# Two mixtures of experts, dense or on sorted rows, in a two-layer recurrent fp32 kernel

## The reference

```python
xn = layernorm(x)                       # x: 16 x 512 x 128
s  = quaternion_stack(xn)               # 4 layers: qkv, Hamilton products, spectral filter, projection, MLP
g  = silu(moe0(xn))                     # 8 experts, hidden 256, each token uses its best 2
x  = x + s * g
xn = layernorm(x)
s  = windowed_attention(xn)             # 16 heads of 64, windows of 128, rotary embedding
g  = silu(moe1(xn))                     # 32 experts, hidden 64, best 4 within 2 of 4 groups, plus a shared expert
x  = x + s * g

# moe0: for every expert e: h = silu(xt @ w_gate[e]) * (xt @ w_up[e]); out += ge[:, None] * (h @ w_down[e])
# moe1: y_e = (silu(xt @ gate_w[e].T) * (xt @ up_w[e].T)) @ down_w[e].T; sum of topk_w * y_e over the chosen 4, + shared
```

## Time and profile before

| | us |
|---|---|
| median of 3 runs | 4817.23 |
| lowest, highest | 4806.15, 4819.19 |
| profiled execution, its own time | 4814.87 |
| its span | 4813.1 |
| PE busy | 4264.2 (89%) |
| DVE busy | 3833.5 (80%) |
| ACT busy | 3274.9 (68%) |
| POOL busy | 1996.1 (41%) |
| a middle round | 287.7 |
| start to the end of the first round | 298.3 |
| last round | 199.5 |

### The profile page before, as it was taken

How to read it: one execution, slowest core, us unless ns; L and a number is a source line. 1 busy time by engine, 2 the same in 40 slices (tenths; PEclk the granted TensorE clock), 3 DMA queues, 4 the chain that set the end, 5 groups by cost and what they waited for, 6 DMA issues and landing times. The chain is left out here.

```text
span 4813.1 us, 75678 instructions
## 1 busy us (share of the span) xinstructions
PE 4264.2 (89%) x20208; PEld 2603.9 (54%) x20208; DVE 3833.5 (80%) x8946; ACT 3274.9 (68%) x6140; POOL 1996.1 (41%) x2033
## 2 busy tenths in 40 slices
PE   5669899898998989899898998989889898998979
PEld 3435555565554555555564554555555564555555
DVE  4779798887978879798887978889798887979853
ACT  2447677676776767677676776767777676777745
POOL 1234344344444444444443434444344443434423
PEclk8779999999999999999999999999999999999989
DMA  4001111111101101111111101101111111111100
GB/s 126 16 25 30 27 30 33 26 32 27 30 25 31 39 21 31 28 29 31 29 31 31 28 23 33 36 21 31 30 28 31 30 31 31 27 27 32 34 20 21
DMA packets 144530, 149.37 MB, mean 31 GB/s; under 512 B 27748, under 2 KB 107932, under 8 KB 143960
## 3 DMA queue, kind: packets, MB, share of 16 engines
q1 hardware_dynamic: 144088, 144.19, 11.5%
HBM read 22.45 MB, written 4.19 MB: 6 GB/s over the span
## 5 line engine op out<-in xcount | busy, mean ns | idle before, releaser
L644 POOL TENSOR_TENSOR s_h<-s_h,ge 128x512 f32<-128x512 f32 x512 | 696.9, 1361 | 1319.2 <-ACT ge L654 1076.0
L952 DVE TENSOR_TENSOR acc<-acc,tmp 128x512 f32<-128x512 f32 x768 | 610.6, 800 | 10.1
L952 DVE TENSOR_TENSOR tmp<-comps 128x512 f32<-128x512 f32 x768 | 605.4, 790 | 8.4
L776 ACT ACTIVATE s_h<-bG 128x512 f32<-128x512 f32 x528 | 314.8, 596 | 434.9 <-DVE hu L1139 226.5
L1371 PE MATMUL bC<-hu,w_d 128*128 128x512 f32 x1056 | 565.3, 617 | 15.7 <-DVE hu L1139 15.7
L753 ACT ACTIVATE probs<-bT,nmax 128x256 f32<-128x256 f32 x1024 | 410.8, 476 | 201.7 <-DVE nmax L1100 199.8
L631 POOL TENSOR_TENSOR rot<-rot,sinT 128x512 f32<-128x512 f32 x256 | 338.1, 1321 | 427.6 <-DMA rot<-raw 426.2
L1100 DVE TENSOR_REDUCE nmax<-bT 128x2 f32<-128x512 f32 x512 | 335.5, 685 | 225.8 <-PE bT L1284 225.2
L1326 PEld LDWEIGHTS bT<-V,probsT 128*128 128x128 f32 x3584 | 430.6, 192 | 101.4 <-issue 56.6
L1139 DVE TENSOR_TENSOR hu<-bU,s_h 128x512 f32<-128x512 f32 x528 | 361.4, 684 | 153.8 <-PE bU L1364 79.5
L1326 PE MATMUL bT<-V,probsT 128*128 128x65 f32 x3584 | 438.7, 274 | 26.7 <-ACT probsT L654 25.6
(11 more groups left out here) (201 smaller groups left out, 9482.7 us busy)
## 6 DMA issues: line engine op xcount, KB each, us to landing
rot<-raw SPq DMA_DIRECT2D x1024, 64.0 KB, 2.0
comps<-comps SPq DMA_DIRECT2D x384, 120.0 KB
x_ld<-in_L_attn_x SPq DMA_DIRECT2D x66, 128.0 KB, 2.2
comps<-comps SPq DMA_DIRECT2D x384, 8.0 KB
out<-O SPq DMA_DIRECT2D x16, 256.0 KB, 2.7
w_a<-in_L_attn_W_qkv SPq DMA_DIRECT2D x1, 1536.0 KB, 14.6
w_fc<-in_L_attn_fc_w SPq DMA_DIRECT2D x1, 1024.0 KB, 9.9
w_g<-in_L_ffn_w_gate SPq DMA_DIRECT2D x1, 1024.0 KB, 5.7
```

The costliest lines, as they stand in the source:

```text
L644: nc.gpsimd.tensor_tensor(s_h[:, :], s_h[:, :], ge[:, :], ALU.mult).then_inc(weighed, 1)
L776: nc.scalar.activation(s_h[:, :], bG[:, :], ACT.Silu).then_inc(silu, 1)
L952: V_.tensor_tensor(dst, i0, i1, op).then_inc(ham[h], 1)
```

## The change

Each mixture now works on the rows that were routed to an expert, and on no others.

- **Sort.** From the hits of the routing, PE counts for each expert and each token how many came before (bf16 matmuls with triangles of ones, `rank` and `base`), and DVE makes of it the slot of every choice, with each expert's rows padded to whole tiles of 128 rows, and the expert's number for each tile (`ids`). There are 15 tiles for mixture 0 and 47 (run as 12 groups of 4) for mixture 1.
- **Scatter.** POOL writes the normalised rows to `xs_d` in DRAM with indirect transfers, one for 128 rows: 8 for mixture 0 and 16 for mixture 1 (L702). SP loads them back in 16 groups of 4 tiles (L632), PE turns them (`xT`), ACT copies them to `xs_f`.
- **Weights by tile.** For every tile SP reads the expert's number into a register and issues a load of that expert's weights: 15 of 393 KB (L650, L651) and 48 of 128 KB (L658, L659), each mixture with three buffers.
- **Units.** A tile of mixture 0 is 4 gate and up matmuls of 128 columns and 2 for down, a group of mixture 1 is 8 of 128 columns (64 x 128 out) and 2 of 256. `hu` has two buffers. The sums go out by `ev` (ACT to `ys`), SP stores them in `ys_d` (L639), POOL gathers the rows again (8 and 16 indirect transfers, L710), and DVE weighs and adds them (`mix`), then ACT takes `silu`.
- **Gone:** the selector matmuls, `ge` and its copies, `s_h * ge` on POOL, the split into three parts, the four kinds of turns named above. `out` gives rows by token (32 matmuls of 128 columns in place of 8 of 512).
- **Start.** Weights come laid out by the host, so PE's turns and the ACT copies at the start go. 4.1 MB of `xs_d` are filled with zeros. The loads of the experts' weights into SBUF go.
- All strings of `ORDER` are new.

The diff, cut to its core (POOL, SP, DVE, PE in this order):

```diff
+TILES0, TILES1 = (SLOTS0 - E0) // P + E0, (SLOTS1 - E1) // P + E1
+GT = 4
+WB0, WB1 = 3, 3
+XB, YB = 4, 2
...
+            def scatter(l, n):
+                pool.wait_ge(sort_step[l], n * SORT_STEPS + 8)
+                pool.sem_inc(pool_go, 1)
+                src = xn if l == 0 else x1n
+                for t in range(NT):
+                    for k in range(KS[l]):
+                        at = t * KS[l] + k
+                        nc.gpsimd.indirect_dma_start(xs_d[l], bass.IndirectOffsetOnAxis(slot[l][:, at:at + 1], 0),
+                                                     src[:, t, :], None).then_inc(scattered[l], 16)
+            def gather(l):
...
+                        nc.gpsimd.indirect_dma_start(yg[l][:, k, t, :], None, ys_d[l],
+                                                     bass.IndirectOffsetOnAxis(slot[l][:, at:at + 1], 0)
...
-                def u_part(name, u):
-                    pool.wait_ge(silu, r.unit + (u + 1))
-                    pool.wait_ge(ge_sb, r.gel + (unit_kind(u)[4] + 1))
-                    nc.gpsimd.tensor_tensor(s_h[:, :], s_h[:, :], ge[:, :], ALU.mult).then_inc(weighed, 1)
...
+                def w_part(name, u):
...
+                        e = sp.value_load(ids[0][0:1, u:u + 1], min_val=0, max_val=E0 - 1)
+                        sp.dma_start(w_e0[:, u % WB0, :], p_e0[e]).then_inc(w_in[0][u % WB0], 16)
+                        return
...
+                    for k in range(GT):
+                        tile = min(n * GT + k, TILES1 - 1)
+                        e = sp.value_load(ids[1][0:1, tile:tile + 1], min_val=0, max_val=E1 - 1)
+                        sp.dma_start(w_e1[:, n % WB1, k, :], p_e1[k % 2][e]).then_inc(w_in[1][n % WB1], 16)
...
+                        V_.tensor_tensor(hu[:, n % 2, :], bG[:, S // 2:], s_h[:, 0:S // 2], ALU.mult).then_inc(h_ready, 1)
...
+                    if name == "mix":
...
+                        dve.wait_ge(gathered[n], 16 * K * NT * (no + 1))
+                        w = weight[n][:, :, :].rearrange("p t k -> p k t").unsqueeze(3).to_broadcast([P, K, NT, D])
+                        g = yg[n][:, :, :, :]
+                        V_.tensor_tensor(g, g, w, ALU.mult).then_inc(mix_step[n], 1)
...
-                        mm(bG[:, :], g, src[:, :], start=True, stop=True).then_inc(g_full, 1)
...
+                            for j in range(2 * HALF0):
+                                ins = mm(bG[:, j * P:(j + 1) * P], w[:, j * P:(j + 1) * P], tok, start=True, stop=True)
...
+                            for j in range(2):
+                                for k in range(GT):
...
+                                    ins = mm(bG[on, at:at + P], w_e1[:, buf, k, j * I1:(j + 1) * I1],
+                                             xs_f[:, g % 2, k * P:(k + 1) * P], start=True, stop=True)
...
```

More of the change, by code:

```diff
@@ L113, in has_work @@
         return False
-    if step[0] == "weight":
-        u = step[1]
-        if engine == "pool":
-            return u < UNITS - 1
-        return u < UNITS - 1 and (u >= UNITS0 or u % HALF0 == 0)
+    if engine == "dve" and step == ("gu", SHARED):
+        return False
     if engine == "act":
-        return step not in [("down", u) for u in range(UNITS) if u not in (UNITS0 - 1, UNITS - 1)] and \
-            (step[0] != "r0" or step[1] == 1)
+        return step[0] != "r0" or step[1] == 1
     return True
@@ new lines, in program, with fill_at @@
+        FILLS = NG + 1
+        BANK = NG + 2
+        PER_B = NG // XB
+        first = Round(0, None, 0, 0, 1, 0)
+        last = Round(None, NB - 1, (NB - 1) * UNITS, (NB - 1) * FILLS, (NB - 1) * BANK + 2, (NB - 1) * PER_B)
+        def middle(i):
+            return Round(i, i - 1, i * UNITS - (UNITS - TILES0), i * FILLS - (FILLS - G0), i * BANK - (BANK - G0 - 2),
+                         i * PER_B - (PER_B - G0 // XB))
+        def fill_at(g):
+            return G0 if g == "shared" else g + (g >= G0)
@@ L453, in rounds, with streams, part_of, part @@
             one(last)
-        def streams(r, a, t, u=None, rt=None):
-            units = units_of(r)
-            def u_part(name, n):
-                if n in units:
-                    u(name, n)
+        def streams(r, a, t, m=None, rt=None, x=None, w=None):
+            def part_of(f):
+                def part(*step):
+                    if in_round(r, step):
+                        f(*step)
+                return part if f is not None else None
             def r_part(name, n):
@@ L534, in _ @@
-            load(w_a1[:, :], w_qkv, loaded["wqkv"])
+            load(w_att[:, :, :, :], attn_w.rearrange("l k t n -> k l t n"), loaded["attn"])
+            load(w_fc[:, :, :], fc_w.rearrange("l k n -> k l n"), loaded["attn"])
+            sp.wait_ge(blank, 1)
+            for l in range(2):
+                n = xs_d[l].shape[0] // P * D
+                width = TOPK1 * NT * D
+                flat = xs_d[l].rearrange("(p a) d -> p (a d)", p=P)
+                for at in range(0, n, width):
+                    end = min(at + width, n)
+                    load(flat[:, at:end], yg[1][:, :, :, :].rearrange("p k t d -> p (k t d)")[:, 0:end - at], zeroed)
@@ L537, in _ @@
             load(cmod[:, :], c_cmod, cs)
+            load(w_mp[:, :, :, :], mproj_w.rearrange("l (a p) n -> p l a n", p=P), cs)
+            load(w_a1[:, :], w_qkv, loaded["wqkv"])
             load(cosT[:, :], c_cos, cs)
@@ L682, in _ @@
             prep_sig(R0_TOP)
-            for h in range(2):
-                prep_gates(h, prep_ready)
             def one(r):
```

819 lines of the change are left out of this document (479 added, 340 removed).

## The result

The changed kernel takes 5234.11 us (median, 5227.76 to 5242.23) against 4815.24 for the kernel before: a ratio of 1.087 (95% interval 1.085 to 1.090). I had forecast 4604. The profiled execution has a span of 5235.3 us, 422 more than before.

What follows compares the result with a forecast made beforehand. The prediction took a chain between DVE and PE as the bound, DVE's 238 us not shrinking. Terms of -12.6 us a round gave 275.1; with start, first and last rounds -211 from 4814.9: 4604 us, range 4520 to 4740.

Steps and rivals of the forecast that it cites:

- PE's work: PE in a middle round: 96 us of matmuls removed, 66.3 added, net -30, to 233 us.
- the clock: PE's granted clock may fall to 0.92: 10 us more PE work a round, of which a third shows.
- Waits of DVE on PE: DVE's waits for PE in a round shrink as mixture matmuls get shorter: -10 us, between 0 and -34.
- The wait on POOL's weighing: DVE's wait for POOL's s_h before hu goes: -4.6 us a round, called certain.
- the port: Port shared by DVE and POOL: POOL's s_h operation leaves, -2 us a round (gain at most 5.0, loss at most 2.2).
- Indirect transfers: 48 a round on POOL at t = 1.3 us each; bursts make gather 1 late, +3 us a round.
- Rival 2: Bursts on POOL: at 2.25 us a transfer, gather 1 and scatter 0 add 22.6 us a round, 4943 us; chance 0.13.
- Register reads on SP: 63 a round ahead of weight loads: 1.0 us a read, 1.6 a tile; SP 5 us late in mixture 1.
- rival 1: SP is the new bound: at 1.5 us a read, 22 us more a round, 4956 us; chance 0.17.
- the 4 us a round at the round's end: End of the round: mix 1 and sort 0 on DVE fall into existing waits, hiding 4 us: -4.
- Rival 3: Small matmuls on PE cost 1.45 times in bulk: +22 us, a round about 285, 4754 us; chance 0.07.
- The port rule: Skill's rule for GpSimd-issued transfers while VectorE holds the shared port: about 0.62 us alone, 3.1 beside a VectorE copy.

Runs made afterwards that it cites:

- e5_both: The changed kernel with no weights fetched in the rounds and plain transfers in place of indirect ones: 4819 us, against 5234 for the changed kernel.
- e13_l0cols: e5_both with 48 in place of 128 columns in the gate and up matmuls of mixture 0 only: 4909 us against 4819.
- e11_warm: e5_both with 16 idle fp32 matmuls of 128 columns added on PE at the start of each round: 4754 us against 4819.
- b2_cols: The kernel before with 352 in place of 512 columns in each gate, up and down matmul of the mixtures: 4781 us against 4815.
- b1_noweigh: The kernel before without POOL's weighing of the units (s_h times ge): 4791 us against 4815.
- e4_plain: The changed kernel with 12 plain transfers a round in place of 48 indirect ones for scatter and gather: 5032 us against 5234.
- e14_nobufwait: The changed kernel with small weight fetches sent to spare DRAM, so SP waits for no free buffer: 5479 us, against 5197 with small fetches that wait.

## Why the prediction was wrong, point by point

Three steps failed, and a fourth in part. The waits of DVE that I let fall with PE's and POOL's work were to give 16.6 us a round, and gave 3.2 where each was tested alone. The fetches cost 15.7 us a round, not 5, and the bursts 11.8, not 3. And the clock fell below the end of my range.

- **PE's work:** 233 us forecast. Measured 252 at a clock of 0.88; at the 0.97 of before that would be 229 (252 x 0.88/0.97, an estimate). The amount was about right, in part by luck, as its terms were not: eight matmuls of 64 output rows take 1.09 us, not 8 x 0.22, four of mixture 0 take 1.16, not 4 x 0.22.
- **The clock:** the term that failed most quietly. I had 0.92 and "a third shows" as an end of my own range. It came to 0.88. In e5_both it moved the time both ways, by +90 us in e13_l0cols and -65 in e11_warm, so less PE work may cost time. What it cost in after itself no run parts from the rest.
- **Waits of DVE on PE, -10 a round:** wrong. Matmuls cut by 27 us in the kernel before give 2.0 (b2_cols). I had divided the waits by PE's load. An in-order engine that waits for others itself has to be followed to what it waits for.
- **The wait on POOL's weighing, -4.6 "with certainty", and the port, -2:** -1.2 together (b1_noweigh). The wait was taken up by the next ones. DVE's operations do get shorter, and by more than I said: those with the same tiles and form, in the same number, take 15.4 us a round less after than before, `acc<-acc,tmp` at 512 columns a mean of 718 ns, not 800. But without the weighing alone it is 4.1 (b1_noweigh). Where the rest comes from, with all strings of `ORDER` new, is not shown. It ends up as idle time.
- **Indirect transfers:** t = 1.3 came out (0.97 + 0.30), by luck, as I had only taken it from another kind of operation. Their place was wrong. I weighed gather 1 and scatter 0. The wait of 6.0 us is at scatter 1, 16 transfers in the middle of layer 0, which I had not put against the root behind it. They are a term mis-sized: I had 3 us a round for all of them; e4_plain gives 11.8, and 27 in the last round, for which I had nothing. Rival 2 named the mechanism, but with a price of 2.25 a transfer as its condition, which was not needed.
- **Register reads on SP:** 1.0 was too much (0.45). Yet rival 1's mechanism is the larger half: 253 us, 15.7 a round where I had 5. I asked whether SP can issue all it has in the stretch; it can. What counts is what stands behind each fetch in the order: four tiles are 3.7 to 4.1 us, and a wait for a free buffer on top, ahead of a roll that DVE needs next. I wrote that it decides from a read of 1.3 us on. That threshold came from throughput and was wrong: a read of 0.45 us was enough.
- **Sum:** without the 8 us a round that I had allowed for fetches and bursts, 120 in 15 rounds, my sum would say 4484. e5_both, which has neither, takes 4819. The 630 us from the forecast to 5234 are thus 335 of base gain that was not there and 415 for fetches and bursts (253 and 202, 40 of it in common), less the 120. If b1_noweigh and b2_cols hold for the new kernel too, the waits explain 13.4 us a round or 201 of the 335 (an estimate). The rest stays open: the 4 us a round at the round's end and the 12 of the last round (it took 202.1 us in e5_both, 199.5 before) were not tested alone, and the clock of e5_both is 0.92, not 0.97.
- **Rival 3** does not carry the result. Its sign was four matmuls of 128 columns at more than 1.2 us: in mixture 0 four take 1.16 us at full clock from the first start to the last end, in mixture 1, with 64 columns of weights, eight take 1.09. Four of `mproj` take a median of 1.11 in the kernel before, so they cost about the same there. The Trainium skill, "TensorE: Matmul & The Clock Gate", "Back-to-back issue gap", which it rested on, has the weight load as part of the spacing at small sizes; the trace agrees in this much, that with 128 columns of weights four 48-column matmuls take 1.09 us, where four of 128 take 1.16.
- **The port rule** of the Trainium skill, "SBUF — State Buffer", in "SBUF: two separate sides" (transfers of GpSimd starve beside VectorE), does not carry the result, though a smaller cost beside DVE shows: inside a burst a transfer takes 0.94 to 0.98 us where DVE is idle, and where DVE is busy a median of 1.02, one in ten over 1.24, the longest 1.97. None takes 3.1.

## What to carry to other kernels

Price a step that is moved onto an in-order queue by what stands behind it there and who needs that next, not by whether the queue's engine has the time: 0.87 us for a tile and 1.27 for a transfer were cheap, and cost 253 and 202 us in all. Work taken off PE is worth only what the chain through the other engines then gives back: measure it with a run that cuts columns and nothing else before building on it. And look at the granted clock of each stretch: where it falls, a few idle matmuls in a wait that PE has anyway can be worth more than work saved.

## What the runs showed of the hardware

- Taking columns from matmuls whose median time does not depend on them (275 ns with 128 or 48) cost 90 us, with a granted clock of 0.88 in place of 0.92 (e13_l0cols), and 16 added matmuls a round gained 65, with 0.94 (e11_warm).
- An indirect transfer of 128 rows of 512 bytes takes POOL a median of 0.97 us and 0.30 to the next, and does not slow DVE as POOL's two-input arithmetic does: `acc<-comps,acc` started at 2294.76, in the middle of a burst, and took 1.23 us, against 2.08 in the earlier trace rows.
- A register read from SBUF on SP takes 0.45 us, and the load behind it 0.34 to issue.
- Bursts of indirect transfers can go together with stalls of up to 14.2 us (e14_nobufwait) of PE, ACT and DVE at once, which no record explains. They end near the burst's last transfer.
